# Row gathers in groups of sixteen, and a rotated product kept in its PSUM bank, in a two-layer adaLN kernel

## The reference

```python
x = L0_attn_query                                   # (4, 1024, 128)
h = layernorm(x) * (1 + ca) + sa                    # layer 0
x = x + ga * linear_attention(h)
h = layernorm(x) * (1 + cb) + sb
x = x + gb * experts_top1(h)                        # 8 experts, 128 -> 512 -> 128
h = layernorm(x) * (1 + ca) + sa                    # layer 1
ct_q = h @ Wd_q + bd_q;  ct_kv = h @ Wd_kv + bd_kv
query = (ct_q @ Wu_q + bu_q) + rope(ct_q @ Wq_r + bq_r)
key   = (ct_kv @ Wu_k + bu_k) + rope(h @ Wk_r + bk_r)
value = ct_kv @ Wu_v + bu_v
x = x + ga * (softmax(query key^T / scale) value @ Wo + bo)   # 16 heads of 8
h = layernorm(x) * (1 + cb) + sb
e = argmax(h @ router.T);  s = sigmoid(max(h @ router.T))     # 16 experts, top 1
gate, up = split((s * h) @ gate_up[e])
shared = silu(h @ Wsg.T) * (h @ Wsu.T) @ Wsd.T
x = x + gb * (shared + (up * silu(gate)) @ down[e])
```

## Time and profile before

| | us |
|---|---|
| median of 3 runs | 1159.34 |
| lowest, highest of them | 1155.55, 1163.48 |
| the profiled execution: its own time | 1156.96 |
| the profiled execution: span, first to last instruction | 1155.1 |
| projections of layer 1, about | 235 to 336 of the span |
| expert loop of layer 1, about | 1036 to 1095 of the span |
| mean granted TensorE clock, share of full speed | 0.962 |

### The profile page before, as it was taken

One profiled execution on the slowest core, in us unless ns is written; L12 is line 12 of the kernel. 1 busy time (PEld: TensorE's weight loads), 2 busy tenths in 40 slices (PEclk: granted clock), 3 DMA queues, 4 the chain that ended last, 5 costly groups with the idle time before them and its releaser, 6 DMA issues. The chain is left out here.

```text
span 1155.1 us, 23773 instructions
## 1 busy us (share of the span) xinstructions
PE 1038.0 (90%) x9049; PEld 497.4 (43%) x9049; DVE 931.4 (81%) x1461; ACT 787.4 (68%) x1536; POOL 318.1 (28%) x460
## 2 busy tenths in 40 slices
PE   6988699577778999999999999999999989999897
PEld 4776598553421222222222222222222239767655
DVE  7887454478778999999999999999999908756445
ACT  4553433144456999999999999999999984535321
POOL 4631377467530000000000000000000007055464
PEclk9999899879877999999999999999999999999999
DMA  7001366316650101111011101110010000713313
GB/s 244 1 22 53 93 193 179 121 26 181 186 190 3 30 3 30 31 30 22 11 30 32 30 3 30 30 30 18 15 30 3 2 3 7 207 36 92 90 53 94
DMA packets 60695, 71.67 MB, mean 62 GB/s; under 512 B 9892, under 2 KB 39716, under 8 KB 60072
## 3 DMA queue, kind: packets, MB, share of 16 engines
q1 hardware_dynamic: 55784, 60.30, 19.1%
q0 software_dynamic: 4800, 9.86, 3.5%
HBM read 45.02 MB, written 25.05 MB: 61 GB/s over the span
## 5 line engine op out<-in xcount | busy, mean ns | idle before, releaser
L1521 DVE TENSOR_REDUCE mx<-p_psA 128x1 f32<-128x1024 f32 x492 | 562.8, 1214 | 11.3 <-PE p_psA L1689 11.1
L1622 ACT ACTIVATE h<-p_psS 128x512 f32<-128x512 f32 x984 | 527.6, 596 | 36.0 <-PE p_psS L1745 21.1
L1776 PE MATMUL p_acc<-h,p_V 128*32 128x256 f32 x4096 | 326.3, 392 | 14.0 <-ACT attn L1600 13.3
L1745 PE MATMUL p_psS<-Q,K 51*128 51x512 bf16 x984 | 302.3, 384 | 0.4 <-DMA Q<-m_rows 0.4
L1689 PE MATMUL p_psA<-K,Q 48*128 48x512 bf16 x984 | 299.3, 386 | 2.6 <-DVE mx L1521 1.7
L1776 PEld LDWEIGHTS p_acc<-h,p_V 128*32 128x32 f32 x4096 | 82.9, 108 | 208.9 <-ACT h L1622 105.0
L1426 POOL TENSOR_TENSOR mr<-zeros,mx 128x16 f32<-128x16 f32 x32 | 7.1, 222 | 542.0 <-DVE mx L1521 532.6
L1689 PEld LDWEIGHTS p_psA<-K,Q 48*128 48x128 bf16 x984 | 54.5, 94 | 208.0 <-DVE mx L1521 159.8
L1745 PEld LDWEIGHTS p_psS<-Q,K 51*128 51x128 bf16 x984 | 59.7, 93 | 10.2 <-ACT h L1622 9.0
L1107 DVE TENSOR_TENSOR f_h<-f_bank,b 128x512 f32<-128x512 f32 x39 | 27.0, 692 | 42.1 <-PE f_bank L1175 42.1
L2157 POOL DMA_INDIRECT h<-hrows,gidx x32 | 32.1, 1003 | 48.1 <-DVE gidx L888 32.2
(11 more groups left out here) (365 smaller groups left out, 1516.7 us busy)
## 6 DMA issues: line engine op xcount, KB each, us to landing
f_w<-in_w SPq DMA_DIRECT2D x39, 256.0 KB, 3.2
Q<-q_rows SPq DMA_DIRECT2D x32, 192.0 KB, 4.7
K<-k_rows SPq DMA_DIRECT2D x32, 192.0 KB, 5.1
result<-f_shared_kept SPq DMA_DIRECT2D x11, 256.0 KB, 2.4
result<-f_y SPq DMA_DIRECT2D x9, 256.0 KB, 3.4
hrows<-h SPq DMA_DIRECT2D x4, 516.0 KB, 7.7
x<-in_x SPq DMA_DIRECT2D x4, 512.0 KB, 5.6
w<-in_w SPq DMA_DIRECT2D x1, 2048.0 KB, 9.3
```

Of the source, the lines that this page charges most:

```text
L1521: dve.tensor_reduce(mx[v % 2][:, h, qt:qt + 1], psA[t][:], AX.X, ALU.max).then_inc(a_max, 1)
L1622: act.activation(pt[s % 2][:, head_at(s, j), :], psS[k % 3][:], ACT.Exp, scale=INV_SCALE).then_inc(s_out, 1)
L1745: pe.matmul(psS[k % 3][:], K[g % NBUF][rows, h // 2, kc * P:(kc + 1) * P], Q[g % NBUF][rows, h // 2, half * 512:(half + 1) * 512], start=T ...
L1776: mm = pe.matmul(acc[VW * h:VW * (h + 1), cols], V[:, v0 + h * (HD + 1):v0 + h * (HD + 1) + VW], pt[s % 2][:, h, cols], start=(kc == 0 and ...
```

## The change

Two edits that have nothing to do with each other.

- A new constant `ROWS_RUN` = 4 takes the place of `RUN` for the row gathers of the last stage: four semaphores in place of two, and POOL waits for all that is in flight before each fourth group, at k = 16 and k = 32, not before each second one. The gathers back of the results keep `RUN` = 2.
- In the projections the first rotated product is written over its own input in PSUM, not into `ras`; the sum reads it from there and writes into `rbs`. `ras` goes.

```diff
 RUN = 2
+ROWS_RUN = 4
...
-        hT, ctT, ras, rbs = late[8:10], late[10:12], late[12:14], late[14:16]
+        hT, ctT, rbs = late[8:10], late[10:12], late[14:16]
...
-                    dve.scalar_tensor_tensor(out=ras[qk], in0=a, scalar=M.bcol1[:, bu + 1:bu + 2], in1=rope[:, 0, j],
+                    dve.scalar_tensor_tensor(out=a, in0=a, scalar=M.bcol1[:, bu + 1:bu + 2], in1=rope[:, 0, j],
...
-                    link(dve.tensor_tensor(ras[qk], ras[qk], rbs[qk], ALU.add))
+                    link(dve.tensor_tensor(rbs[qk], psR[qk][1], rbs[qk], ALU.add))
...
-                    dve.scalar_tensor_tensor(out=full[:, qk, :], in0=u, scalar=M.bcol1[:, bu:bu + 1], in1=ras[qk],
+                    dve.scalar_tensor_tensor(out=full[:, qk, :], in0=u, scalar=M.bcol1[:, bu:bu + 1], in1=rbs[qk],
...
-        got = [n.sem(f"got{i}") for i in range(RUN)]
+        got = [n.sem(f"got{i}") for i in range(ROWS_RUN)]
...
-                    if k % GT == 0 and q >= RUN and q % RUN == 0:
+                    if k % GT == 0 and q >= ROWS_RUN and q % ROWS_RUN == 0:
                         for landed in got:
-                            pool.wait_ge(landed, 16 * GT * (q // RUN))
+                            pool.wait_ge(landed, 16 * GT * (q // ROWS_RUN))
```

## The result

| | before | changed |
|---|---|---|
| median, us | 1159.37 | 1148.28 |
| lowest, highest, us | 1153.27, 1167.04 | 1144.24, 1155.23 |
| runs | 18 | 18 |
| span of the profiled execution, us | 1155.1 | 1144.1 |

The ratio is 0.9902 with a 95% interval of 0.988 to 0.9923: 11.1 us less where 7.9 were forecast. The interval is 8.9 to 13.9 us less, so the shortfall of the forecast is more than noise.

The account below looks back on a forecast made before the run. POOL's row gathers were taken to bound the last stage, PE's pace lying close below, with DVE lacking slack in the projections. Terms -5.9 and -2.0 took 1156.96 to 1149.1, or 1151.4 as median; range 1146 to 1159.5.

Parts of the forecast that it names:

- The loop, -5.9: Last stage's expert loop: with three gather waits gone, PE keeps its 4.19 us pace and group 11 starts 5.86 us earlier.
- group 10's cover: Expert loop: group 10's rows arrive at 1078.16, PE needs them at 1078.71, half a microsecond to spare.
- POOL's side, -6.33: Row gathers: waits before k = 8, 24 and 40 go, saving POOL 6.33 us; those at 16 and 32 stay.
- The clock fall, 1.3 of the 5.9: Expert loop: beyond waits of 2.15 + 2.39, the gain is avoiding the clock's fall to 0.62 behind the first wait.
- Rival B: Expert loop: POOL gains but PE does not follow; some 3 of the 5.9 us stay, 1154.4; chance 0.12.
- The rotated product, -2.0: Projections: the add with one PSUM input no longer excludes POOL and runs at 0.69 us; 2.0 us saved, bounds 0 to -3.6.
- the 1.1 forecast: Projections before the wait at 296.75: 0.80 us from the first blocked add plus some 0.3 us that POOL no longer loses.
- The in-place write, 0: Projections: writing the product into its own PSUM bank costs nothing; bounds -0.8 to +8.4 us over sixteen.
- Rival C: Projections: the in-place write takes its bank twice per element, +8.4 us, 522 ns each; slower, 1159.8; chance 0.06.
- Rival A: Only the gathers pay, 1153.4: a PSUM operand costs 52 ns at both changed instructions, or a DMA wait stays; chance 0.21.
- its other half: Projections: the alternative ground for only the gathers paying, that the DMA wait at 296.75 does not move.
- D with luck: All add blocks count (-3.6) and POOL's full 6.3 is taken, 1149.4, chance 0.07; over 1% faster needs luck besides.

Follow-up runs that it names:

- the product alone: Changed kernel with ROWS_RUN = 2, so only the rotated product in PSUM differs from the kernel before: 1156.03 us, ratio 0.9975.
- groups of four: Changed kernel with ROWS_RUN = 1, POOL waiting before every group of four row gathers, eleven waits instead of two: 1159.22 us, ratio 1.0016.
- The three comparisons: Changed kernel, unaltered, measured three times against the kernel before: 1148.28 us (ratio 0.9902), 1150.25 us and 1147.65 us (0.9895).
- the results' gathers: Changed kernel with ROWS_RUN also used for the gathers back of the results, one wait instead of three: 1149.58 us, ratio 0.9905.
- groups of thirty-two: Changed kernel with ROWS_RUN = 8, the wait at k = 16 gone too and only that at k = 32 left: 1150.37 us.

## Why the prediction was right, and where it was short

- **The loop, -5.9: right, by its own steps.** Measured 5.87 between groups 7 and 11 and 5.8 on the whole in the first pair, 6.1 as a mean over twelve profiles. PE's steps of 4.19, the clock at 1.00, no wait at group 8 or 10, all as written; group 10's cover held but for 0.11 us in one of nine profiles. "From the first gather to the loop's last group 67.7" was measured as 67.8.
- **POOL's side, -6.33: too small.** First to last gather took 62.7, not 64.1. I counted three waits gone and left the two others as they were, but they shrank too: the gap at k = 16 went from 3.64 to 3.27 us, that at k = 32 from 3.87 to 3.35; and one stray gap of 1.70, behind the eleventh gather, is not there. PE does not take it, so it touched nothing.
- **The clock fall, 1.3 of the 5.9: right in the mean, luck in its place.** It comes behind the first wait alone in the first profile of the kernel before, behind both in the second, behind the third with the product alone, behind the second of five with groups of four. Each fall costs 1.2 to 1.6 us. Rival B's "the clock falls elsewhere in the loop" is true of five profiles in nine, for some 1.1 us each, not the 3 I gave it.
- **The rotated product, -2.0: the right mechanism; its parts were counted too small.** L1474 is at 0.69 in all sixteen while L1447 in the same run is not. Three things were off. "13.8 - 16 x 0.692 = 2.7 us too much" was read from a single execution, the mildest of four (2.7, 6.6, 4.7, 4.6): the excess hangs on which add meets which POOL subtraction. "Behind 296.75 the last two adds count, 1.15 instead of 0.69 each" missed one. DVE's timeline of the kernel before has three:

```profile
318.38 1.15 DVE L1473 TENSOR_TENSOR attn<-attn 128x512 f32<-128x512 f32 x1
...
328.37 1.15 DVE L1473 TENSOR_TENSOR attn<-attn 128x512 f32<-128x512 f32 x1
...
333.05 1.15 DVE L1473 TENSOR_TENSOR attn<-attn 128x512 f32<-128x512 f32 x1
```

  That is 1.4 us behind the wait, not 0.92, and -2.5 in all. And the term had no share for the clock and for PE. In the first pair the way from the first add to the end of the wait at 296.75 (293.65 in the changed kernel) shrank by 1.3 us, close to the 1.1 forecast (51.6 to 50.3), though the wait itself grew from 3.70 to 4.59. Behind it 2.3 us went (36.3 to 34.0), more than all the excess that lay there; DVE's waits for PE over the stretch were 3.0 shorter, and the clock was 0.94, not 0.88. How much of this the shorter adds brought and how much is luck with the clock stays open. Over all profiles the stretch is 3.2 us shorter, or an estimated 2.3 at an equal clock. Neither is clear of the 2.0 forecast by the scatter.
- **The in-place write, 0: right.** 751 and 753 ns in the mean against 744 and 748, 0.1 us over sixteen. Rival C falls with it: reading and writing one bank in one instruction costs 5 to 7 ns here, not 522. Rival A's 52 ns fall as well, at the add (692 against 692) and at the product, and so does its other half, since the gather at 296.75 came earlier. With the 52 ns falls what VectorE: DVE Perf Modes of the Trainium skill ("The TRN2 errata") would have made of the add: its 120 fixed cycles for a source in PSUM against 58 would show as an estimated 65 ns, and no such difference is in any run here. What that skill's SBUF — State Buffer says ("SBUF: two separate sides"), that a DVE operation with two SBUF inputs and a GpSimd operation that reads SBUF block each other, the trace bears out: the add at 253.40, with one input in PSUM, is not delayed, L1447 at 266.98, with two in SBUF, is.
- **The sum.** The terms as measured are -6.1 and -3.2, together -9.3, where -7.9 was forecast. The three comparisons gave -11.1 (8.9 to 13.9), -8.8 (5.6 to 11.2) and -11.0 (9.3 to 14.9). All three agree with -9.3, the third only just; -7.9 lies outside the first and the third. In the first pair of profiles 1.8 us more lie ahead of both edits: the first rotated add starts at 243.3 instead of 245.1, and anywhere from 242.3 to 250.3 over all profiles, with no instruction changed before it. In the three where it starts last (249.2 to 250.3) the granted clock from 60 to 120 us was 0.86, but it was 0.86 in one that starts at 246.9 too, and 0.89 to 0.97 in the other nine. What sets the start stays open.
- **The chances.** I gave 0.07 to faster by over 1% because "D with luck" was needed. The measured 0.9902 stands on that bound. With the excess taken as uncertain by its own kind (which adds are hit differs from execution to execution) the chance should have been higher; by how much no run here says.

## What to carry to other kernels

Price a drained queue by who waits for it: here each full wait costs POOL about 2 us, but it is worth that only where the consumer has caught up (groups 8 and 10), and nothing where it is behind (the results' gathers, groups of thirty-two). Where the cost of an instruction depends on what another engine does at that moment, one profile gives one draw; take its excess as a range from that up to every instance being hit before sizing the gain, and compare profiles at an equal clock. Here a DVE add that reads one input from PSUM was free of POOL at no price in its own length, and writing the operand back into its bank cost 5 to 7 ns.

## What the runs showed that I had not expected

- A SCALAR_TENSOR_TENSOR that reads a PSUM bank and writes over it (128x512 f32) takes 751 to 753 ns in the mean, 5 to 7 more than with its output in SBUF (744 and 748).
- The granted clock is not settled by the wait ahead of it. It fell behind waits of 2.15, 2.18, 2.35, 2.37 and 3.29 us, and not behind 2.27, 2.31, 2.39 and 2.40; in other executions of the same loop it fell at its start. (The waits of 0.62, 1.23 and 1.52 us had no fall behind them either.)
- The excess that POOL adds to one and the same DVE line was 2.7 us in one execution of the kernel before and 6.6 in another: the 3.9 between them are more than the 3.0 us that the edit alone brought.
- Taking away the DMA wait in front of DVE (4.59, 2.70 and 3.40 us in the changed kernel's three profiles) gave nothing that shows: the adds took 84.6 us with it gone, at a clock of 0.88. DVE's four additions behind it took 2.04 us instead of 1.14, and its waits for PE 5.1 instead of 1.2.
